# Attention block: key-query scores by seven half-size products, and output added in DRAM by DMA

## The reference

```
h = group_norm(x) * gn_w + gn_b;  q, k, v = split(qkv_w @ h + qkv_b)
attn = softmax(q^T k / sqrt(512));  o = attn @ v
out = x + out_w @ o + out_b        # x: [16, 512, 32*32]
```

## Time and profile before

| | |
|---|---|
| median of 3 runs | 2134.47 us (2133.47 to 2136.08) |
| the profiled execution's own time | 2135.79 us |
| its span | 2132.8 us |
| PE busy | 2118.6 us, 99% |
| DVE / ACT / POOL busy | 65% / 38% / 13% |
| mean granted TensorE clock | 0.999 |

### The profile page before, as it was taken

One profiled execution on the slowest core, in us unless ns is written; L12 is line 12 of the kernel. 1 busy time (PEld: TensorE's weight loads), 2 busy tenths in 40 slices (PEclk: granted clock), 3 DMA queues, 4 the chain that ended last, 5 costly groups with the idle time before them and its releaser, 6 DMA issues.

```text
span 2132.8 us, 23156 instructions
## 1 busy us (share of the span) xinstructions
PE 2118.6 (99%) x9340; PEld 1752.8 (82%) x9340; DVE 1382.1 (65%) x1885; ACT 801.5 (38%) x1179; POOL 275.2 (13%) x109
## 2 busy tenths in 40 slices
PE   8999999999999999999999999999999999999999
PEld 6788888888888888888888888888888888888887
DVE  6683766848567485675847758476683866748555
ACT  6441614426143351533515244162442614326141
POOL 2020111101111011110111102011020111101110
PEclk9999999999999999999999999999999999999999
DMA  5101020010201101010010200102001020110001
GB/s 165 41 21 60 2 79 2 30 50 2 79 2 35 46 10 70 2 56 25 16 65 2 79 2 21 60 2 79 2 30 50 2 79 2 35 45 6 35 1 40
DMA packets 48635, 76.16 MB, mean 36 GB/s; under 512 B 20400, under 2 KB 21136, under 8 KB 48528
## 3 DMA queue, kind: packets, MB, share of 16 engines
q1 hardware_dynamic: 47664, 72.32, 9.8%
q0 software_dynamic: 864, 2.36, 0.6%
HBM read 38.32 MB, written 33.98 MB: 34 GB/s over the span
## 4 chain that ended last, share of the span: by engine, by line
PE 97%; POOL 0%; DVE 0%; issue 0%; DVEq 0%; POOLq 0%
PE ring L194 32%; PE ring L196 32%; PE ring L195 32%; POOL xs L484 0%; DVE tv_lo L640 0%; DVE xs L590 0%; DVE key_raw L593 0%; DVE xs L702 0%; DVE ring L696 0%; POOL bqk L498 0%; DVE keybias L595 0%; DVEq L695 0%; POOLq L142 0%
## 5 line engine op out<-in xcount | busy, mean ns | idle before, releaser
L194 PE MATMUL ring<-h_hi,tv_hi 128*128 128x512 f32 x1024 | 399.2, 390 | 1.9 <-DVE tv_lo L640 1.9
L196 PE MATMUL ring<-h_hi,tv_lo 128*128 128x512 f32 x1024 | 399.0, 390 | 0.0
L195 PE MATMUL ring<-h_lo,tv_hi 128*128 128x512 f32 x1024 | 398.9, 390 | 0.0
L194 PE MATMUL ring<-p_hi,tv_hi 128*128 128x512 f32 x1024 | 398.3, 389 | 0.0
L195 PE MATMUL ring<-p_lo,tv_hi 128*128 128x512 f32 x1024 | 398.3, 389 | 0.0
L196 PE MATMUL ring<-p_hi,tv_lo 128*128 128x512 f32 x1024 | 398.3, 389 | 0.0
L419 ACT ACTIVATE tv_hi<-ring,t_bias 128x512 fp32r<-128x512 f32 x128 | 88.3, 690 | 660.3 <-PE ring L196 660.3
L398 ACT ACTIVATE stage<-ring,keybias 128x512 f32<-128x512 f32 x256 | 173.5, 684 | 275.3 <-PE ring L196 266.0
L403 ACT ACTIVATE stage<-stage 128x512 f32<-128x512 f32 x256 | 161.6, 631 | 209.3 <-DVE stage L661 209.3
L194 PEld LDWEIGHTS ring<-h_hi,tv_hi 128*128 128x128 f32 x1024 | 192.6, 188 | 41.9 <-DVE tv_lo L640 1.9
L640 DVE SCALAR_TENSOR_TENSOR tv_lo<-ring,t_bias,tv_hi 128x512 fp32r<-128x512 f32 x128 | 95.4, 750 | 201.3 <-ACT tv_hi L419 196.7
(11 more groups left out here) (103 smaller groups left out, 2910.7 us busy)
## 6 DMA issues: line engine op xcount, KB each, us to landing
xs<-x_in SPq DMA_DIRECT2D x64, 512.0 KB, 5.9
out<-xs SPq DMA_DIRECT2D x128, 256.0 KB, 2.0
xs<-xs POOLq DMA_DIRECT2D x3, 512.0 KB, 8.3
xs<-wk SPq DMA_DIRECT2D x4, 256.0 KB, 3.8
xs<-wq SPq DMA_DIRECT2D x4, 256.0 KB, 5.0
stage<-wv SPq DMA_DIRECT2D x4, 256.0 KB, 8.0
stage<-wo_t SPq DMA_DIRECT2D x4, 256.0 KB, 9.1
stage<-stage POOLq DMA_DIRECT2D x3, 256.0 KB, 3.4
```

The lines of the kernel that those rows point to most:

```text
L194: nc.tensor.matmul(ps_out, st_hi, m_hi, start=first, stop=False)
L195: nc.tensor.matmul(ps_out, st_hi, m_lo, start=False, stop=False)
L196: return nc.tensor.matmul(ps_out, st_lo, m_hi, start=False, stop=last)
```

## The change

1. The scores of a batch are computed as a 2x2 block product in Strassen-Winograd form. T is cut in quarters by channels and key halves (A11, A12, A21, A22), h by channels and query halves. Sums of quarters are formed on DVE (S1 to S4 of T, `t_sum`; t1 to t4 of h, `h_combined`), each is split in hi and lo, and seven products of 4 tiles by 6 matmuls take the place of 192 matmuls: 168. A product's unit is 6 matmuls long (28 units). Products that belong together accumulate in the same PSUM bank, banks 0 to 3 for A11, S2, S3, A22 and banks 4 to 7 for A12, S1, S4; ACT copies the bank between two of them (`copy_scores`) and DVE adds the other bank (`add_scores`). All seven are taken for the tiles i = 0 and 1, then for i = 2 and 3.
2. The ring of 7 banks is gone: units have fixed banks among 8. V unit m uses bank m, output unit (nb, c) bank 4 nb + c, T unit j bank j.
3. The output is not added to x on the core. ACT adds the output bias to x in place (`shift_input`), SP stores that, and the next image is loaded into the same buffer. DVE scales the output from PSUM into one of three SBUF buffers, and POOL issues a DMA that adds it to what was stored (`add_output`).
4. Softmax sums are all trees on DVE (`sum_tree`); exponentials, maxima's subtraction, hi and lo parts go by two tiles (1024 elements); reciprocals are taken on [128, 4] after a way through DRAM, and the key bias is spread through DRAM too.
5. DVE's and ACT's orders are rewritten. Both score halves end nearly together, and the whole softmax follows.

```diff
-T0, S0, S1, V0, A0, UNITS = 0, 8, 16, 24, 32, 40
-RING = 7
+T0, S0, V0, A0, UNITS = 0, 8, 36, 44, 52
+PRODUCTS = [(A11, "b11"), (A12, "b21"), (S1, "t1"), (S2, "t2"), (S3, "t3"), (A22, "t4"), (S4, "b22")]
...
+            def score_products(b):
+                for pair_of, (p, (a, name)) in itertools.product(range(2), enumerate(PRODUCTS)):
+                    own_bank = p in (P_A12, P_S1, P_S4)
+                    for i in (2 * pair_of, 2 * pair_of + 1):
...
+                        elif p == P_A22:
+                            pe.wait_ge(s_p3, b * 4 + i + 1)
...
+                        for kk in range(2):
+                            m = three(at, ..., opens and kk == 0, kk == 1, not opens)
+                        m.then_inc(s_unit, 1)
...
             def output_units(b, nb):
                 for c in range(CT):
+                    pe.wait_ge(s_vlo, b * 8 + CT * nb + c + 1)
                     for m in range(MT):
                         if c == 0:
                             if nb == 0:
                                 pe.wait_ge(s_vlo, b * 8 + m + 1)
-                            pe.wait_ge(s_plo, b * 16 + nb * MT + m + 1)
+                            pe.wait_ge(s_plo, b * 8 + nb * CT + m // 2 + 1)
...
             # ACT, inside the pair loop of the scores
+                    for i in pair_of:
+                        copy_scores(b, P_S2, i, i, 8 + i, s_p2)
+                    if pair_of[0] == 0:
+                        shift_input(b, 2)
+                        shift_input(b, 3)
+                    for i in pair_of:
+                        copy_scores(b, P_S3, i, CT + i, 12 + i, s_p3)
...
             # POOL
             def max_all(b, nb):
+                lone_wait(pool, s_rmax[nb], (b + 1) * 7)
+                if nb == 1:
+                    pool.wait_ge(s_sub, b * 8 + CT)
...
+            def add_output(b, nb, c):
+                pool.wait_ge(s_scaled, n + 1)
+                nc.gpsimd.dma_start(out_v[b, :, c, here], scaled[n % 3][:, :],
+                                    accum_op=ALU.add).then_inc(s_added[n % 3], DMA)
...
             # DVE, after the last score tiles
+                subtract_max(b, 0, 0)
+                subtract_max(b, 0, 1)
                 v_rest(b, 0)
+                p_rest(b, 0, 0)
+                subtract_max(b, 0, 2)
                 v_rest(b, 1)
+                p_rest(b, 0, 1)
+                subtract_max(b, 0, 3)
+                v_rest(b, 2)
...
+                v_rest(b, 4)
+                if more:
+                    group_spread(b + 1)
+                sum_tree(b, 0)
+                v_rest(b, 5)
+                subtract_max(b, 1, 0)
+                subtract_max(b, 1, 1)
+                v_rest(b, 6)
+                v_rest(b, 7)
```

More of the change, by code:

```diff
@@ L178, in _ @@
                     group_stats(b + 1)
[L179 to L187, removed]
+                own_sums(b, 0)
@@ L188, in _ @@
+                spread_inverses(b, 0)
+                own_sums(b, 1)
+                spread_inverses(b, 1)
+                if b + 1 < B:
+                    key_bias(b + 1)
             for k in range(CT):
-                sp.wait_ge(s_stored[k], B * NB * DMA)
+                sp.wait_ge(s_sent[k], B * DMA)
+            for y in range(3):
+                sp.wait_ge(s_added[y], (B * 8 - y + 2) // 3 * DMA)
         @block.tensor
         def _(pe):
[L193 to L196, removed]
@@ L220, in weight_vector, with product_step @@
                 a.then_inc(s_vec, 1)
[L222 to L230, removed]
+            def product_step(w, k, banks, between=None):
                 pe.wait_ge(s_wlo[w], k + 1)
@@ L381, in _ @@
             for k in (0, 2, 1, 3):
-                weighted_rows(1, ((1, BV),), k)
+                nc.scalar.activation(wo_rows[k][:, :], raw[1][:, 2 * k + 1, :], ACT.Identity,
+                                     scale=col[:, BV + k:BV + k + 1]).then_inc(s_rows[1], 1)
             for i in range(CT):
-                product_part(1, i, u_hi, bank(i - CT))
+                product_part(1, i, u_hi, ring[:, u_bank[i], :])
+            for c in range(CT):
+                h_combined_part(0, c)
@@ new lines, in t_direct_part, with t_sum_part @@
+            def t_direct_part(b, a, kk):
+                j = {A22: 2, A11: 4, A12: 6}[a] + kk
+                i = T_ORDER[j][0]
+                act.wait_ge(s_unit, b * UNITS + T0 + j + 1)
+                nc.scalar.activation(t_part(r_hi, a, kk), ring[:, t_bank(b, j), :], ACT.Identity,
+                                     bias=t_bias[:, i:i + 1]).then_inc(s_thi, 1)
+            def t_sum_part(b, a, kk):
+                act.wait_ge(s_tsum, b * 8 + T_SUM[a][kk])
+                nc.scalar.activation(t_part(r_hi, a, kk), stage[:, t_full[a] + kk, :], ACT.Copy).then_inc(s_thi, 1)
@@ new lines, in copy_scores, with shift_input @@
+            def copy_scores(b, p, i, m, to, done):
+                act.wait_ge(s_unit, b * UNITS + score_unit(p, i) + 1)
+                nc.scalar.activation(stage[:, to, :], ring[:, i, :], ACT.Identity,
+                                     bias=keybias[:, m:m + 1]).then_inc(done, 1)
+            def shift_input(b, k):
+                if b == 0 and k == 0:
+                    act.wait_ge(s_vec_sb, 3)
+                nc.scalar.activation(xs[:, k, :], xs[:, k, :], ACT.Identity,
+                                     bias=out_bias[:, k:k + 1]).then_inc(s_shifted, 1)
@@ new lines, in _, with t_direct_rest @@
+            dve.wait_ge(s_vec, 3)
+            nc.vector.tensor_tensor(out_bias[:, :], ps_ob, col[:, BO:BO + CT], ALU.add).then_inc(s_vec_sb, 1)
+            for c in range(CT):
+                h_combined_rest(0, c)
+            dve.wait_ge(s_bqk, 1)
+            def t_direct_rest(b, a, kk):
+                j = {A22: 2, A11: 4, A12: 6}[a] + kk
+                i = T_ORDER[j][0]
+                dve.wait_ge(s_thi, b * 14 + 2 * a + kk + 1)
+                nc.vector.scalar_tensor_tensor(t_part(r_lo, a, kk), ring[:, t_bank(b, j), :], t_bias[:, i:i + 1],
+                                               t_part(r_hi, a, kk).bitcast(FP32), ALU.add,
+                                               ALU.subtract).then_inc(s_tlo, 1)
@@ new lines, in max_step @@
+            def max_step(b, nb, step, m, ready, count):
+                dve.wait_ge(ready, count)
+                first = stage[:, (0, 12)[nb], :]
+                if step == 1 and b > 0:
+                    dve.wait_ge(s_added[nb], (b * 8 - nb + 2) // 3 * DMA)
+                if step > 1:
+                    dve.wait_ge(s_rmax[nb], b * 7 + step - 1)
+                    first = run_max[nb][:, :]
+                nc.vector.tensor_tensor(run_max[nb][:, :], first, stage[:, 8 * nb + m, :], ALU.max).then_inc(s_rmax[nb], 1)
```

761 lines of the change are left out of this document (451 added, 310 removed).

## The result

| | before | after |
|---|---|---|
| median | 2134.89 us (2133.47 to 2136.08) | 2244.62 us (2241.51 to 2247.83) |
| span of the profiled execution | 2132.8 us | 2241.4 us |
| mean granted TensorE clock | 0.999 | 0.961 |

The ratio is 1.051, interval [1.050, 1.053]: 5% slower. 2236 was forecast.

What follows compares the result with a forecast made beforehand. PE, busy 99% of the span, was taken as the bound: 2135.8 - 87.1 + 18.4 + 133.5 + 3.9 + 25.5 + 7 + 0.7 = 2237.7, against the median 2236 us; 8 in 10: 2150 to 2290.

Steps and rivals of the forecast that it cites:

- The matmuls, -87.1: All 16 batches: 24 matmuls fewer in each, 384 x 0.2267 us, saving 87.1 us if no wait is added.
- V and the first output unit, 133.5: First output unit: PE waits for late lo parts of V, 8.9 us in each of 15 batches, 133.5 us.
- the clock, 25.5: Nearly idle PE around the first output unit drops to 1.2 GHz: 1.7 us for 15 batches, 25.5 (0 to 51).
- Scores, 18.4: Scores, first pair of tiles: two shift_input delay S3's copy, PE waits before A22, 1.15 us a batch, 18.4 us.
- Beside the maximum's reduction, 0.6: End of scores: DVE's last maximum step is delayed 0.6 us (0 to 1.2) by POOL's first maximum reduction.
- Head, +7: First batch: h's sums and lo parts on DVE delay products A11 and A12, +7 us (-2 to +15).
- Tail, +0.7: End of run: scaled output lands by POOL's DMA (3.4) instead of an addition and a store, +0.7 us.
- last batch, 3.9: Last batch, with no next image and no group_rstd: V7 at about 30.3, PE wait 3.9 us.
- The exponential at 1.06: Softmax on ACT: a 1024-wide exponential costs as a copy, 1.06 us (range 0.63 to 1.26).
- A: Rival on POOL's code load before group_rstd: it does not hold DVE, wait 5.0 us, clock up, 2152 us; chance 0.13.
- B: Rival, last maximum to V7: DVE-ACT alternation looser, V7 by E+27 (E: scores' end), faster, 2073 us fully hidden; chance 0.08.
- C: Rival on the output: accumulating DMA beyond 13 us to landing makes PE wait in T, 2349 us at 20; chance 0.04.

Runs made afterwards that it cites:

- e6: The changed kernel with the edits of e2, e3 and e4 together: 2065.2 us, 0.967 of the kernel before.
- e1: The changed kernel with DVE taking group_spread (and affine_pair) after V7's lo part instead of ahead of the sum tree: 2191.4 us, ratio 1.026.
- e2: The changed kernel with hi and lo parts of V5 to V7 ahead of group_spread, sum tree and the second half's first exponential: 2108.7 us, ratio 0.987.
- e3: The changed kernel with all four shift_input of ACT ahead of the copies of S2: 2241.5 us, ratio 1.050.
- e10: e6 with h_combined_rest and the output bias ahead of key_dot in the first batch: 2062.5 us, ratio 0.966.
- e4: The changed kernel with group_rstd between POOL's two maximum reductions and a one-column reduction behind it: 2219.9 us, ratio 1.039.
- e5: e4 with POOL's first sum reduction also waiting for DVE's first two subtractions of the second half: 2191.0 us, ratio 1.026.
- e7: The changed kernel with e2's and e3's edits and h_combined_rest ahead of key_dot in first batch and loop: 2137.4 us, ratio 1.001.

## Why the prediction was right

Its sum was 2237.7 against 2243.2 for the profiled execution (span 2241.4), and its large term stands, by mechanism and by size. That the total came so near is in part luck: scores and output stage took some 5 us less than their terms, head, tail and last batch 11 us more. Step by step:

- **The matmuls, -87.1.** Right: 8956 of them, and e6 gets the gain once nothing waits.
- **V and the first output unit, 133.5, with the clock, 25.5.** Forecast 10.6 us a batch, measured 10.35. The chain named is the one found: code load 6.74 behind the second maximum, DVE's wait 3.47 (forecast 3 to 4), tree, V5, then V6 behind ACT's exponential. e1 takes the code load's part out and gets 53 us, e2 takes the whole out. V5 came a little earlier than walked: two waits of 4.4 and 2.9 us, where I had 5.0 and 3.9 with 0.7 between. The second is shorter also because PE ran slowly between them, three matmuls in place of 0.7 us taking 1.65. Of the clock I had 1.7 a batch; 119 matmuls at 0.2 us more are 24 us, 1.6.
- **Scores, 18.4.** Measured 0.98 a batch, 15.7; e3 confirms the mechanism, since without the shifts the wait is gone. But its removal isn't worth that: e3 gained 3.1. The sum treated the terms as independent, and the place of the slow stretch links them.
- **Beside the maximum's reduction, 0.6.** The first maximum step beside it takes 1.05 instead of 0.69 us:

```profile
387.65 1.05 DVE L871 TENSOR_TENSOR run_max<-run_max,stage 128x512 f32<-128x512 f32 x1
```

  0.36, inside the 0 to 1.2 that I gave. The Trainium skill's rule (SBUF — State Buffer, Who interferes with whom), by which the second to start blocks until the first is finished, would have made it 1.2; the trace agrees that the operation is held up and disagrees on how long.
- **Head, +7.** Mis-sized, though inside -2 to +15: PE's wait there is 14.8 us against 1.88 of idle before, so 12.9, or 13.9 with the slow matmuls. I priced the lo parts of h's sums at 1.2 us each and left out the delay beside a reduction, though I had it two paragraphs above; they ran beside POOL's and four took 8.95:

```profile
50.67 8.95 DVE L761 TENSOR_TENSOR r_lo<-stage,r_hi 128x1024 fp32r<-128x1024 f32 x4
```

  e10 gives them back their 4.63, and PE's wait shrinks by 2.8.
- **Tail, +0.7, and last batch, 3.9.** 1.8 and 7.2. In the last batch I had no clock term, and not the meeting of the sum reduction with two subtractions (shown under e4), 1.8 us. The accumulating DMA lands in 4.3 us, not 3.4, and the small DMA to `inv` in 3.6, not 2.0, which cost PE no wait (medians, the page after, answers to the earlier trace rows):

```profile
out<-run_max POOLq DMA_DIRECT2D x86, 256.0 KB, 4.3
inv<-inv_row SPq DMA_DIRECT2D x32, 256.0 KB, 3.6
```

- **The exponential at 1.06.** Right, 1058 ns (groups by line, against the earlier trace rows):

```profile
L518 ACT ACTIVATE stage<-stage 128x1024 f32<-128x1024 f32 x128 | 135.5, 1058 | 403.6 <-DVE stage L878 401.8
```

**The rivals.** A is ruled out, since DVE does wait for the load (3.47). Its price was too low too: e1 and e5, where DVE doesn't wait, are 2191. A's text had the clock stay up there, but behind the one wait of 3.5 us nine matmuls ran at the lower level. B: its mechanism isn't there, V6's hi part waits for the exponential as walked; its idea, the V parts out of that path, is e2. C: no wait of PE in T in after, and 4.3 us is far from 13. But its place was real: in e7 DVE waits 5.0 us for such a buffer, with the DMA held not by DRAM but by the reduction ahead of it on POOL.

## What to carry to other kernels

Fewer matmuls pay only if every consumer's operands are still there in time: walk each in-order engine from the last input of a stage to the first operand of the next, and put what PE wants next ahead of what it wants in 40 us (e2, 136 us for a few moved lines). Where PE pauses elsewhere in the batch, a wait's worth is not its length: take all waits out before judging one edit (e3 alone 3 us; in e6 S3's 12.9 us of waits are gone and nothing comes back in their place). On POOL count what is queued behind a reduction or a code load, transfers among it, and what runs on DVE beside it.

## What the runs showed of the hardware

- **A pause costs twice.** Behind PE waits of 3.5 to 5.5 us in the loop, every time in these runs, matmuls start 0.43 us apart (granted clock 0.50, the 1.2 GHz level) for 3 to 5 us, then 0.227 again. Behind waits of 2.8 us it went either way: in e7 the clock fell at eleven of them and stayed up at four. At the 1.1 to 1.8 us waits of e2 and the 0.8 us ones of the scores it stayed up, but it fell once behind 1.88 us. How many matmuls are slow depends on where in the wait the clock falls: 119 in after (2.0 to 2.9 us after PE stops), 174 in e3 (3.5 to 4.6 us). What sets that moment I leave open.
- **DVE and POOL hold each other up, in part.** A partition reduction of 3.24 us makes two subtractions take 4.14 instead of 2.35 (e4, e5), the 6.11 us one makes four lo parts take 8.95 instead of 4.63 (after, e10), and the other way one reduction, started 0.06 us behind an operation of DVE, took 4.27 instead of 3.24 (423.25 in after). So a reduction holds such an operation up for half to seven tenths of its own length: at the maximum until 388.01, 0.88 of 1.79 us in, and beside the lo parts for 4.3 of 6.11. The Trainium skill (SBUF — State Buffer, Who interferes with whom) calls the shared ports an exclusive lock; held for the whole reduction it would cost more than any of these rows shows.
- **POOL's change of code is paid on each switch.** 6.74 and 7.00 us ahead of `group_rstd`, 5.96 back to the reduction; the first alone is 103 us in 15 batches on POOL. The Trainium skill (GPSIMD Engine Reference, Instruction dispatch) gives some 6 us for the first call to a freshly loaded kernel; the trace agrees in size, and shows it again in every batch.
